# An LSTM over 512 steps on one core: the O gate computed with its weights stationary, and TensorE's order of work within a step changed

## What is computed

```
xW = jnp.einsum('ntd,dk->tnk', x, Wx) + b
c0 = zeros
def step(carry, xw_t):
    prev_h, prev_c = carry
    a = xw_t + prev_h @ Wh                  # (4, 1024): i, f, o, g, 256 columns each
    i, f, o = sigmoid(a[:, 0:256]), sigmoid(a[:, 256:512]), sigmoid(a[:, 512:768])
    g = tanh(a[:, 768:1024])
    next_c = f * prev_c + i * g
    next_h = o * tanh(next_c)
    return (next_h, next_c), next_h
_, hs = scan(step, (cond, c0), xW)          # 512 steps, one after the other
return x + transpose(hs, (1, 0, 2))
```

## Time and profile before

| | us |
|---|---|
| time, 3 runs | median 1089.95 (1089.76 to 1093.87) |
| the profiled execution: its own time | 1090.95 |
| the profiled execution: span from first to last instruction | 1089.2 |
| busy PE, PE weight loads, DVE, ACT | 697.3, 574.9, 790.8, 550.4 |
| mean granted clock of TensorE | 0.963 of full |

### The profile page before, as it was taken

One profiled execution on the slowest core, in us unless ns is written; L12 is line 12 of the kernel. 1 busy time (PEld: TensorE's weight loads), 2 busy tenths in 40 slices (PEclk: granted clock), 3 DMA queues, 4 the chain that ended last, 5 costly groups with the idle time before them and its releaser, 6 DMA issues.

```text
span 1089.2 us, 88137 instructions
## 1 busy us (share of the span) xinstructions
PE 697.3 (64%) x36864; PEld 574.9 (53%) x36864; DVE 790.8 (73%) x4897; ACT 550.4 (51%) x3586; POOL 0.7 (0%) x6
## 2 busy tenths in 40 slices
PE   4666666666666666666666666667666666766664
PEld 3555555555555555555555555555555555545554
DVE  4777777777777777777776777776777777777776
ACT  2455555555545555555554555554545555455554
POOL 0000000000000000000000000000000000000000
PEclk9999999999999999999998999998999998999999
DMA  3000000000000000000000000000000000000000
GB/s 89 5 7 5 6 6 6 6 6 5 7 5 6 7 5 5 6 6 6 6 6 6 5 6 7 5 6 6 6 6 6 6 6 6 5 6 6 6 6 7
DMA packets 32110, 8.74 MB, mean 8 GB/s; under 512 B 31584, under 2 KB 31584, under 8 KB 32096
## 3 DMA queue, kind: packets, MB, share of 16 engines
q1 hardware_dynamic: 31488, 8.41, 3.5%
q10 hardware_dynamic: 608, 0.14, 0.1%
HBM read 6.43 MB, written 2.10 MB: 8 GB/s over the span
## 4 chain that ended last, share of the span: by engine, by line
DVE 51%; PE 24%; ACT 14%; issue 8%; SPq 1%; DVEq 1%; DMA 0%
DVE turned_bank L296 39%; PE gates L364 24%; DVE h_pad L314 8%; ACT tanh_o L212 8%; ACT turned_bank L215 7%; DVE scan_both L301 3%; DVE cell L307 1%; DVEq L330 1%; SPq L139 1%; DVE h_rows L270 0%; DMA wh_raw<-in_L_cond_Wh_dram 0%; SPq L143 0%; DVEq L269 0%; DVE wh L225 0%; DVE wh L222 0%
## 5 line engine op out<-in xcount | busy, mean ns | idle before, releaser
L364 PE MATMUL gates<-wh,h_pad 128*32 128x64 f32 x32768 | 591.2, 227 | 374.8 <-DVE h_pad L314 373.3
L364 PEld LDWEIGHTS gates<-wh,h_pad 128*32 128x32 f32 x32768 | 506.5, 114 | 488.3 <-DVE h_pad L314 486.4
L296 DVE STREAM_TRANSPOSE turned_bank<-gates 128x64 f32<-128x64 f32 x2048 | 478.5, 262 | 182.3 <-PE gates L364 170.0
L203 ACT ACTIVATE tanh_f<-turned_bank 128x8 f32<-128x8 f32 x512 | 90.7, 177 | 438.1 <-DVE turned_bank L296 427.6
L210 ACT ACTIVATE scan_both<-turned_bank 128x8 f32<-128x8 f32 x1024 | 185.1, 181 | 59.9 <-DVE turned_bank L296 17.3
L314 DVE SCALAR_TENSOR_TENSOR h_pad<-tanh_o,turned_bank 128x4 f32<-128x4 f32 x1024 | 132.7, 158 | 74.2 <-ACT turned_bank L215 4.6
L307 DVE TENSOR_TENSOR_SCAN cell<-scan_both 128x12 f32<-128x12 f32 x1024 | 144.0, 181 | 2.1 <-issue 0.3
L215 ACT ACTIVATE turned_bank<-cell 128x4 f32<-128x4 f32 x1024 | 143.3, 172 | 2.5 <-DVE cell L307 0.3
L346 PE MATMUL x_acc<-wx,x_units 128*32 128x128 f32 x2048 | 107.5, 285 | 9.3 <-DVE x_units L249 9.3
L212 ACT ACTIVATE tanh_o<-turned_bank 128x8 f32<-128x8 f32 x512 | 90.7, 177 | 28.9 <-DVE turned_bank L296 6.7
L216 ACT ACTIVATE half_d<-cell 128x8 f32<-128x8 f32 x512 | 100.4, 196 | 0.0
(11 more groups left out here) (24 smaller groups left out, 6.7 us busy)
## 6 DMA issues: line engine op xcount, KB each, us to landing
x_next<-in_x_dram SPq DMA_DIRECT2D x256, 8.0 KB
x_here<-in_x_dram SPq DMA_DIRECT2D x256, 8.0 KB
out_dram<-y_rows SPq DMA_DIRECT2D x256, 8.0 KB
wx_raw<-in_L_cond_Wx_dram SPq DMA_DIRECT2D x8, 128.0 KB, 3.4
wh_raw<-in_L_cond_Wh_dram SPq DMA_DIRECT2D x8, 128.0 KB, 2.7
bias_raw<-in_L_cond_b_dram ACTq DMA_DIRECT2D x4, 32.0 KB, 3.1
h_rows<-in_cond_dram ACTq DMA_DIRECT2D x4, 1.0 KB
```

The lines of the kernel that those rows point to most:

```text
L203: nc.scalar.activation(tanh_f[:], of_step(BF, t), ACT.Tanh).then_inc(tanh_f_done, 1)
L296: nc.vector.transpose(turned[k], gates[k][:, 0:W]).then_inc(gates_turned[k], 1)
L364: last = nc.tensor.matmul(gates[k][q * R:(q + 1) * R, 0:W], h_stationary(b, t), wh[:, b, q, columns_of(k)], start=False, stop=b == M - 1, ...
```

## The change

F, the two G and I banks stay by rows and turned by VectorE. The O gate is now built by units: the weights are the stationary operand (32 columns of `wh`) and h, four columns wide, the moving one, so the result has units on partitions and needs no turn. Each half of O has a PSUM bank of its own (`o_units`), to which ScalarE's tanh goes directly, one instruction per half in place of one for both. The x part of O must lie by units as well: VectorE turns 64 columns of `x_part` once a chunk (`turn_x_part`, ahead of step 7), and TensorE injects them in step 0 (`inject_units`). `make_x_part` moves from step 7 to step 6, and the x product is made in two pieces of 256 columns behind steps 3 and 4 where it was four of 128 behind steps 3 to 6. TensorE takes half 0 of h for F and for the first G and I bank, then waits for half 1. The turned gates and `tanh_c` lie in SBUF, where they lay in PSUM. The second scan no longer waits for `forgotten`.

```diff
-    BF, BA, BB, BO = range(4)
+    BA, BB, BF, BO = range(4)
+    ROWS = (BF, BA, BB)
...
-    PIECES = [(b, slice(c * GC // 2, (c + 1) * GC // 2)) for b in range(M) for c in range(2)]
-    FIRST_PIECE_AT = 3
+    X_PRODUCT_AT = (3, 4)
+    X_PART_AT = STEPS - 2
+    UNIT_COLUMNS = slice(GC - 2 * R, GC)
...
-        turned_bank = [ps(f"turned_bank{k}", [128, 512]) for k in range(3)]
-        turned = [turned_bank[k][:, 0:W] for k in (0, 1, 2)] + [turned_bank[0][:, W:2 * W]]
-        tanh_c = [turned_bank[AB[m]][:, W:W + N] for m in range(M)]
+        turned = {k: sb(f"turned{k}", [128, W]) for k in ROWS}
+        tanh_c = [sb(f"tanh_c{m}", [128, N]) for m in range(M)]
...
-                    act.wait_ge(gates_turned[BO], now)
-                    nc.scalar.activation(tanh_o[:], of_step(BO, t), ACT.Tanh)
                     for m in range(M):
+                        act.wait_ge(o_done[m], now)
+                        nc.scalar.activation(tanh_o[:, m, :], o_units[m][:, t * N:(t + 1) * N], ACT.Tanh).then_inc(o_tanh_done, 1)
                         act.wait_ge(cell_done[m], now)
-                        nc.scalar.activation(tanh_c[m], cell[:, m, :, K - 1], ACT.Tanh, scale=0.5).then_inc(tanh_done[m], 1)
+                        nc.scalar.activation(tanh_c[m][:], cell[:, m, :, K - 1], ACT.Tanh, scale=0.5).then_inc(tanh_done[m], 1)
...
+            def turn_x_part(chunk):
+                dve.wait_ge(x_part_made, chunk + 1)
+                nc.vector.transpose(x_part_units[:], x_part[:, UNIT_COLUMNS]).then_inc(x_part_turned, 1)
...
-                    dve.wait_ge(forgotten, now)
+                    if m == 0:
+                        dve.wait_ge(forgotten, now)
...
                 forget()
-                turn(BO)
                 update(0)
...
+            def inject_units(bank, k, m):
+                at = k * W + m * R - UNIT_COLUMNS.start
+                for q in range(Q):
+                    nc.tensor.matmul(bank[q * R:(q + 1) * R, 0:R], ident[:, q * R:(q + 1) * R],
+                                     x_part_units[:, at:at + R], start=True, stop=False,
+                                     tile_position=(0, q * R), skip_group_check=True)
...
+                def units(b, bank, k, m):
+                    at = k * W + m * R
+                    for q in range(Q):
+                        last = nc.tensor.matmul(bank[q * R:(q + 1) * R, t * N:(t + 1) * N], wh[:, b, q, at:at + R],
+                                                h_at(b, t - 1), start=False, stop=b == M - 1,
+                                                tile_position=(0, q * R), skip_group_check=True)
+                    return last
...
                 pe.wait_ge(h_done[0], now)
-                recur(0, BF)
+                rows(0, BF)
+                rows(0, BA)
                 pe.wait_ge(h_done[1], now)
-                recur(1, BF).then_inc(gates_done[BF], 1)
-                for k in (BA, BB, BO):
-                    recur(0, k)
-                    recur(1, k).then_inc(gates_done[k], 1)
-                if t == STEPS - 1 and ahead:
-                    pe.wait_ge(x_part_made, chunk + 2)
-                    for k in BANKS:
+                rows(1, BF).then_inc(gates_done[BF], 1)
+                rows(1, BA).then_inc(gates_done[BA], 1)
+                rows(0, BB)
+                rows(1, BB).then_inc(gates_done[BB], 1)
+                if t == 0:
+                    for m in range(M):
+                        inject_units(o_units[m], BO, m)
+                for m in range(M):
+                    units(0, o_units[m], BO, m)
+                    units(1, o_units[m], BO, m).then_inc(o_done[m], 1)
+                if ahead and t in X_PRODUCT_AT:
+                    x_product(X_PRODUCT_AT.index(t), chunk + 1)
+                if ahead and t == STEPS - 1:
+                    for k in ROWS:
                         pe.wait_ge(gates_turned[k], now)
-                        inject(k)
-                if ahead and 0 <= t - FIRST_PIECE_AT < len(PIECES):
-                    x_product(*PIECES[t - FIRST_PIECE_AT], chunk + 1)
+                    pe.wait_ge(x_part_turned, chunk + 2)
+                    inject_early()
```

More of the change, by code:

```diff
@@ L63, in lstm_residual_kernel @@
         x_part = sb("x_part", [128, GC])
+        x_part_units = sb("x_part_units", [128, UNIT_COLUMNS.stop - UNIT_COLUMNS.start])
         tanh_f = sb("tanh_f", [128, M, N])
@@ L75, in lstm_residual_kernel @@
         y_rows = sb("y_rows", [128, QD])
-        gates = [ps(f"gates{k}", [128, 512]) for k in BANKS]
+        gates = {k: ps(f"gates{k}", [128, 512]) for k in ROWS}
+        o_units = [ps(f"o_units{m}", [128, 512]) for m in range(M)]
         x_acc = ps("x_acc", [128, 512])
-        turned_bank = [ps(f"turned_bank{k}", [128, 512]) for k in range(3)]
-        turned = [turned_bank[k][:, 0:W] for k in (0, 1, 2)] + [turned_bank[0][:, W:2 * W]]
-        tanh_c = [turned_bank[AB[m]][:, W:W + N] for m in range(M)]
+        turned = {k: sb(f"turned{k}", [128, W]) for k in ROWS}
+        tanh_c = [sb(f"tanh_c{m}", [128, N]) for m in range(M)]
         wx_loaded = [sem(f"wx_loaded{b}") for b in range(M)]
@@ L99, in lstm_residual_kernel @@
         x_part_made = sem("x_part_made")
+        x_part_turned = sem("x_part_turned")
         h_turned_back = sem("h_turned_back")
@@ L102, in lstm_residual_kernel @@
         y_stored = sem("y_stored")
-        gates_done = [sem(f"gates_done{k}") for k in BANKS]
-        gates_turned = [sem(f"gates_turned{k}") for k in BANKS]
+        gates_done = {k: sem(f"gates_done{k}") for k in ROWS}
+        gates_turned = {k: sem(f"gates_turned{k}") for k in ROWS}
+        o_done = [sem(f"o_done{m}") for m in range(M)]
         tanh_f_done = sem("tanh_f_done")
+        forgotten = sem("forgotten")
         tanh_ig_done = [sem(f"tanh_ig_done{m}") for m in range(M)]
         kept_done = sem("kept_done")
-        forgotten = sem("forgotten")
+        o_tanh_done = sem("o_tanh_done")
         cell_done = [sem(f"cell_done{m}") for m in range(M)]
@@ L256, in _ @@
             make_x_part(0)
+            turn_x_part(0)
             permute_matrix(wh, wh_raw, 1, 0.5, wh_loaded).then_inc(wh_made, 1)
@@ L290, in step @@
                     nc.vector.transpose(x_units[:], x_next[:]).then_inc(x_turned, 1)
-                if ahead and t == STEPS - 1:
+                if ahead and t == X_PART_AT:
                     make_x_part(chunk + 1)
+                if ahead and t == X_PART_AT + 1:
+                    turn_x_part(chunk + 1)
                 def turn(k):
                     dve.wait_ge(gates_done[k], now)
-                    nc.vector.transpose(turned[k], gates[k][:, 0:W]).then_inc(gates_turned[k], 1)
+                    nc.vector.transpose(turned[k][:], gates[k][:, 0:W]).then_inc(gates_turned[k], 1)
                 def forget():
```

37 lines of the change are left out of this document (19 added, 18 removed).

## The result

The changed kernel takes 1122.99 us (median of 4 runs, 1122.59 to 1124.04); the ratio to the kernel before, which took 1091.15 beside it, is 1.029, 95% interval 1.0266 to 1.0314. The forecast was 1121. Its sum was right and its split was not: the path between the engines took about twice what I gave it, and the clock a quarter.

A forecast was written before the change was run, and what follows sets the result against it. No engine is full; the loop from h to h, run 512 times, bounds the kernel. 1090.95 us plus 6 (SBUF), 6 (step 0) and 19 (clock), less 1 between profile and median, gave 1121 us; range 1077 to 1178.

The forecast's parts named there:

- O's turn at 0: VectorE: O's turn lies in the shadow between forget product and scan, so removing it is worth 0.
- the rival in which the chain of waits was right: VectorE: O's turn was on the path, so 36 us less; 1086 or 1045 us; chance 0.07.
- TensorE's new order at 0: TensorE: bank B complete after 12 groups as before; F's turn at 0.61, its tanh ready exactly when the forget product starts.
- SBUF at +0.012: Turned gates and cell tanh in SBUF: together +0.011 a step, +6 us, bounds -5 and +17 us.
- Half 1 of h: covered: ScalarE's order moves half 1 to about 0.19 behind half 0; TensorE's four groups on half 0, 0.25 us, cover it.
- Step 0 at +0.09: Turning back of h and F's turn in step 0 move by 0.09 with half 1: some +6 us.
- Chunk work at 0: X product pieces, x part, its extra turn and O's injection stand in engines' idle time: 0; uncovered, 29 us.
- The stall of step 4 stays: VectorE's unexplained stall in step 4, 0.12 us on the period, stays; -8 or +8 us allowed.
- The clock at +19: TensorE's lower clock falls in nearly every chunk: 60 stretches at 0.73, 44 us in place of 25, +19 us.
- The lower clock didn't stick: Rival on TensorE's clock: it stays low until an x product comes, 1165 to 1200 us; chance 0.20.
- O was never waited for: Rival that O comes late: slow small matmuls make its half 1 ready at 1.9, 1220 us; chance 0.03.
- the clock got worse: Judges the rival that TensorE's clock is not worse, small matmuls counting like wide ones: 1077 to 1096 us; chance 0.20.

The follow-up runs named there:

- run 9: Kernel before without VectorE's turn of O; tanh of O reads the bank of gates as it lies, giving other values of O: 1086.9 us, ratio 0.992.
- run 10: Kernel before with only the change's order on TensorE (F and first G and I bank with half 0, then both with half 1): 1077.59 us, ratio 0.984.
- run 4: Changed kernel with the cell tanh back in PSUM, turned gates staying in SBUF: 1121.14 us, ratio 1.026.
- run 11: Kernel before with turned F, G and I and the cell tanh in SBUF, O's turn staying in PSUM: 1097.78 us, ratio 1.001.
- run 5: Changed kernel with both tanhs of O ahead of both cell tanhs on ScalarE: 1123.26 us, ratio 1.027.
- run 7: Changed kernel with cell tanh in PSUM, both tanhs of O ahead of the cell tanhs, and F of both halves first on TensorE: 1122.04 us, ratio 1.026.
- the three edits: On the changed kernel: cell tanh in PSUM, both tanhs of O ahead of the cell tanhs, F of both halves first; alone 1122.04 us, ratio 1.026.
- run 2: Changed kernel with one dummy 256-column matmul behind O in the six steps without an x product: 1104.31 us, ratio 1.010.
- run 3: Kernel before with the same kind of dummy matmul behind the gates of steps 0 to 2: 1067.97 us, ratio 0.978.
- run 12: Changed kernel with the three edits and the dummy matmul in steps 0, 1, 2, 5 and 6, two signals moved: 1061.72 us, ratio 0.970.
- run 8: Changed kernel with the three edits and the dummy matmul in steps 0 to 2: 1120.77 us, ratio 1.025.

## Why the prediction was right or wrong

**What bounds the kernel, O's turn at 0.** Right, and shown by run 9: without the turn a step is as long as with it. That settles the rival in which the chain of waits was right.

**TensorE's new order at 0, "the last slack of F is used up".** The mechanism was right, the size wrong. I put the forget product's start as a tie and stopped there. It isn't only when it starts: let go by its own wait it lasts 0.17, and behind a turn 0.15 (0.13 behind one into SBUF). Run 10: +0.017 a step.

**SBUF at +0.012** (cell tanh 0.015, tanh of F 0.005, h -0.008). The cell tanh is 0.03 (run 4 takes just that out of the step, 2.08 to 2.05). The product that makes h takes 164 ns with its tanh in SBUF, 158 with it in PSUM, where I had booked a gain of 0.008. The term that I mis-sized most is the product of the two edits. SBUF alone makes a step 2.02 to 2.04 (run 11), the order alone 2.03 (run 10), and both 2.08, where their sum would be 2.04 to 2.06. With F early, a turn into SBUF brings the scan 0.024 closer to the start of the forget product (0.231 in place of 0.255). With F late, that gain is gone (0.273). And tanh of F, 208 ns in place of 177, goes on the path; the turn of F into SBUF is 0.015 shorter, so the forget product starts 0.016 later. The two edits ran together only inside the changed kernel, beside O's. So +0.067 a step in place of +0.011.

**Half 1 of h: covered.** Right (run 5).

**Step 0 at +0.09.** Too much: 2.10 against 2.08, 0.02 to 0.03. Since every step now waits for F, the delay of step 0's F adds only what exceeds the rest's. It came from half 1, as forecast: with half 1 earlier it is gone (run 5).

**Chunk work at 0.** Right: steps 3, 4, 6 and 7, which hold it, last 2.08 at full clock like the others.

**The stall of step 4 stays.** Wrong for the changed kernel: a chunk lost the 0.16 us of stalls that it had in steps 4 and 6 (2.13 and 2.06 before, 2.08 after), -10 us. Path in all: 34 + 1.5 - 10 = 25, the 24 of the chunk.

**The clock at +19.** The cost of a stretch was right, 0.73 against 0.78. Their number was not: 39, not 60. I took it that less work on TensorE makes the clock fall in nearly every chunk. Runs 4, 7 and 10 show that this is not enough: the same matmuls in steps that differ by 1% gave 23 or 4 stretches (clock 0.963 and 0.994), and the three edits, which add or remove no matmul, raised 39 to 69 (0.895). With more of TensorE's time filled in the right steps the falls end (runs 2, 3, 12); in the wrong steps they don't (run 8). That work in TensorE's idle time prevents the falls is shown; that little work alone brings them is not, since 2.033 us steps escape them where 2.016 us ones don't, with less work per us. Why they do stays open. My time came out by luck: two errors of 13 and 14 us had opposite signs. Of the signs of being right that I had named, F's turn at 0.61 and B's at 0.95 came; others didn't: a mean clock of 0.94 and not 0.90, steps of 2.08 and not 2.02 to 2.04, 0.27 and not 0.25 from forget product to scan.

**The other rivals.** The lower clock didn't stick: of 33 low stretches 30 lasted 3.4 us. O was never waited for. And the clock got worse, so the small matmuls didn't keep it up as the wide ones had.

## What to carry to other kernels

When two edits both use up the slack of one operand, price them together: each alone cost 0.01 to 0.02 us in an ordinary step here, both 0.067. In a chain of short bursts on TensorE, look at the granted clock before anything on the path: 25 to 62 us of 1100 hung on it, it took back nearly all that the path edits of runs 4 and 7 had gained, and one wide dummy matmul in the idle time of each poorly filled step, placed by where this kernel's own clock falls, got it back. Judge a path edit by the length of a full-clock step, and only then by the time.

## What the runs showed that I had not expected

- A loop body of 348 matmuls on TensorE ran on 10 instruction packets, one of 420 on 202, with stops of up to 5 us, and took 1364 us or more in place of 1123.
- The same VectorE operation had three lengths, by what let it go: the forget product lasted 0.17 behind its own wait, 0.15 behind a turn into PSUM, 0.13 behind one into SBUF.
- The cell tanh, SBUF to SBUF, takes 202 ns on average, to PSUM 174. The page "ScalarE: Activation LUTs" of the Trainium skill (What ACT_TABLE_LOAD costs) would give 189, an estimate; the trace decides.
- A step stalls by 0.04 to 0.15 at a fixed place of the loop that moves with the code: step 4 before (and 0.04 in step 6), step 6 in run 9, step 5 in run 12, none in the changed kernel. I have no cause for it.
